# Two layers of a transformer on one core: a new order and new skews for the stages of the token pipeline, and two PSUM banks handed over one by one

## What is computed

```python
h = _layernorm(x, axis=-1) * (1 + ca) + sa
x = x + ga * _L0_attn_ref(h, L0_attn_qkv, L0_attn_wo)            # causal attention, 16 heads
h = _layernorm(x, axis=-1) * (1 + cb) + sb
x = x + gb * _L0_ffn_ref(h, L0_ffn_W_r, ...)                     # r * (relu(k)**2 @ W_v), each token mixed with the one before
...                                                              # the second layer's six vectors
h = _layernorm(x, axis=-1) * (1 + ca) + sa
x = x + ga * _L1_attn_ref(h, L1_attn_Wq, ...)                    # a scan over the tokens, + residual, its own layernorm
h = _layernorm(x, axis=-1) * (1 + cb) + sb
x = x + gb * _L1_ffn_ref(h, L1_ffn_router_w, ...)                # h + shared MLP + the best 2 of 16 experts
```

## Time and profile before

| | before |
|---|---|
| median of 3 runs | 2248.11 us (2240.46 to 2248.99) |
| the profiled execution | 2240.73 us, span 2239.0 us |
| TensorE busy in the span | 1976.6 us (88%) |
| VectorE, ScalarE, GpSimd busy | 1711.7, 1423.5, 927.1 us |
| the token pipeline, first transpose to the first expert's | 1363.68 to 1877.10 us of the span |
| the experts, from there | 361.90 us |

### The profile page before, as it was taken

The page is one execution under the profiler, slowest core; times in us unless marked ns, Lnnn a source line. Parts: engine busy times, 40 slices in busy tenths (PEclk is TensorE's granted clock), DMA queues, the critical chain, the costliest instruction groups (busy, mean ns, idle before and its releaser), DMA issues. The chain is left out here.

```text
span 2239.0 us, 30470 instructions
## 1 busy us (share of the span) xinstructions
PE 1976.6 (88%) x10427; PEld 841.6 (38%) x10427; DVE 1711.7 (76%) x2505; ACT 1423.5 (64%) x1913; POOL 927.1 (41%) x818
## 2 busy tenths in 40 slices
PE   7979999989999999999999995888888766999997
PEld 4442222222222222222222213555555434776775
DVE  6779999999999999999999994567777644333332
ACT  5759999989999889999899992454444211111110
POOL 5853444333334433444333431365554431333423
PEclk9989999999999999999999997999999878999999
DMA  6642311031111221143300001101000022443441
GB/s 206 209 137 43 53 22 32 3 64 22 31 22 31 46 43 31 22 127 117 94 24 13 22 22 44 38 19 48 29 29 28 21 82 75 102 110 97 108 99 24
DMA packets 124926, 133.74 MB, mean 60 GB/s; under 512 B 35289, under 2 KB 119090, under 8 KB 124080
## 3 DMA queue, kind: packets, MB, share of 16 engines
q1 hardware_dynamic: 110192, 117.86, 19.3%
q0 software_dynamic: 14592, 14.08, 3.6%
HBM read 96.85 MB, written 50.63 MB: 66 GB/s over the span
## 5 line engine op out<-in xcount | busy, mean ns | idle before, releaser
L1062 DVE SCALAR_TENSOR_TENSOR arena<-ps_s,arena 128x1024 f32<-128x1024 f32 (+1 forms) x1071 | 1147.1, 1139 | 40.9 <-ACT arena L1028 33.0
L1028 ACT ACTIVATE arena<-ps_s 128x1024 f32<-128x1024 f32 (+1 forms) x1194 | 1041.2, 935 | 115.6 <-PE ps_s L975 103.6
L975 PE MATMUL ps_s<-arena 128*128 128x512 bf16 (+3 forms) x2304 | 607.9, 366 | 87.4 <-DVE arena L1062 69.2
L991 PE MATMUL ps_o<-arena,values 128*32 128x512 f32 (+3 forms) x4608 | 565.7, 568 | 5.2 <-ACT arena L1018 3.9
L1071 POOL TENSOR_SCALAR arena<-arena 128x512 f32<-128x512 f32 x123 | 236.1, 1919 | 514.0 <-ACT arena L1033 513.9
L975 PEld LDWEIGHTS ps_s<-arena 128*128 128x128 bf16 x2304 | 155.1, 97 | 694.0 <-DVE arena L1062 531.3
L1805 ACT ACTIVATE arena<-t_ps_four 128x320 f32<-128x320 f32 (+1 forms) x96 | 42.0, 438 | 322.2 <-PE t_ps_four L1697 322.2
L2130 POOL DMA_INDIRECT out<-values,slot_ids x80 | 123.8, 1547 | 238.2 <-DVE values L2051 209.9
L1697 PE MATMUL t_ps_four<-arena 128*128 128x320 f32 (+1 forms) x768 | 211.0, 434 | 0.6 <-DVE arena L2012 0.6
L991 PEld LDWEIGHTS ps_o<-arena,values 128*32 128x32 f32 x4608 | 94.0, 108 | 233.1 <-issue 185.4
L2024 DVE TENSOR_TENSOR arena<-t_ps_four,arena 128x320 f32<-128x320 f32 (+1 forms) x96 | 47.2, 492 | 168.2 <-ACT arena L1805 168.2
(11 more groups left out here) (203 smaller groups left out, 1762.9 us busy)
## 6 DMA issues: line engine op xcount, KB each, us to landing
arena<-parts_dram SPq DMA_DIRECT2D x320, 64.0 KB, 2.2
parts_dram<-arena SPq DMA_DIRECT2D x32, 384.0 KB, 3.4
arena<-parts_dram SPq DMA_DIRECT2D x24, 512.0 KB, 7.0
slots_in_dram<-in_empty_slots SPq DMA_DIRECT2D x10, 1040.0 KB, 24.8
arena<-slots_in_dram SPq DMA_DIRECT2D x16, 650.0 KB
arena<-in_L_ffn_w_gate SPq DMA_DIRECT2D x16, 352.0 KB, 3.1
arena<-in_L_ffn_w_up SPq DMA_DIRECT2D x16, 352.0 KB, 3.7
arena<-in_L_attn_x SPq DMA_DIRECT2D x8, 512.0 KB, 4.3
```

The lines of the kernel that those rows point to most:

```text
L975: last = pe.matmul(ps_s[:, unit.bank + i, p.at:p.at + p.width], m.k_stack[:, group.g % 2 * HG + p.head, p.kt * P:p.kt * P + P], q_stack[:, ...
L991: last = pe.matmul(ps_o[32 * p.head:32 * p.head + 32, p.w0:p.w0 + p.width], m.values_flat[:, at:at + 32], probs[:, job.at % PROB_BANKS, p. ...
L1028: act.activation(probs[:, unit.slot:unit.slot + n], ps_s[:, unit.bank:unit.bank + n], ACT.Exp, scale=1.0 / DH ** 0.5).then_inc(exped, 1)
L1062: dve.scalar_tensor_tensor(p, ps_s[:, unit.bank:unit.bank + n], 0.0, p, ALU.not_equal, ALU.mult).then_inc(bank, 1)
```

## The change

Three things change in `phase_tokens`. The lists of all four engines have a new order. Some skews are new: `turn_attended` with its modulation and `difference` 1 to 2; `spread` 1, `take_keys` 1 and both scans 3 to 4; `delta_out` 3 to 4; `count`, `choose`, `find_places`, `open_up` 2 and `hide` 2 5 to 6; `rows_final` 4 to 5; `scatter` 5 to 7; `normalise_mixed` 3 to 2. And the two banks of `ps_turn` get a pair of counters each: transposes, `up` products, copies, modulations and the two products of `hide` wait for and hand back one bank at a time. `take_attn` becomes two activations of one bank each, where it was one over both; no other operation is added or removed. New waits keep the single buffer `silu` safe (`open_up` waits for the `hide` before it).

```diff
-    turns = Uses(mixed=3, up0=5, up1=5, attn=0, final=4, up2=5, attended=1)
-    outs = Uses(down=6, attend=1, gate=2, value=2, logits=5, count=5, delta=3)
-    banks = Uses(keys=2, spread0=3, spread1=3)
+    turns = Uses(attended=2, mixed=3, up0=5, up1=5, attn=0, final=4, up2=5)
+    outs = Uses(count=6, delta=4, down=6, attend=1, gate=2, value=2, logits=5)
+    banks = Uses(spread1=4, keys=2, spread0=3)
...
-        turned, turn_taken = sem("turned"), sem("turn_taken")
+        turned = [sem("turned0"), sem("turned1")]
+        turn_taken = [sem("turn_taken0"), sem("turn_taken1")]
...
             def turn(name, b, rows):
-                if turns.before(name, b):
-                    pe.wait_ge(turn_taken, turns.before(name, b))
                 for k in range(KC):
+                    if turns.before(name, b):
+                        pe.wait_ge(turn_taken[k], turns.before(name, b))
                     for t in range(TT):
                         last = pe.transpose(ps_turn[:, k, t * P:t * P + P], rows[:, t, k * P:k * P + P], m.ident[:])
-                last.then_inc(turned, 1)
+                    last.then_inc(turned[k], 1)
...
             def up(b, i):
                 at, width = FM[i]
-                pe.wait_ge(turn_taken, turns.before(f"up{i}", b))
                 for half, w in enumerate((m.s_gate, m.s_up)):
+                    pe.wait_ge(turn_taken[half], turns.before(f"up{i}", b))
                     for k in range(KC):
                         last = pe.matmul(ps_turn[0:width, half], w[:, k, at:at + width], m.h_even[:, k, b * BT:b * BT + BT],
                                          start=k == 0, stop=k == KC - 1)
-                last.then_inc(turned, 1)
+                    last.then_inc(turned[half], 1)
...
             def take_attn(b):
-                act.wait_ge(turned, turns.through("attn", b))
                 if b:
                     act.wait_ge(out_made[1], outs.through("attend", b - 1))
-                act.activation(attnT, ps_turn[:], ACT.Copy).then_inc(turn_taken, 1)
+                for k in range(KC):
+                    act.wait_ge(turned[k], turns.through("attn", b))
+                    act.activation(attnT[:, k], ps_turn[:, k], ACT.Copy).then_inc(turn_taken[k], 1)
 
             def modulate(name, b, out, layer, shift, scale):
-                act.wait_ge(turned, turns.through(name, b))
                 for k in range(KC):
-                    last = act.activation(out[:, k], ps_turn[:, k], ACT.Identity, bias=m.mod_cols[:, layer, shift, k:k + 1],
-                                          scale=m.mod_cols[:, layer, scale, k:k + 1])
-                last.then_inc(turn_taken, 1)
+                    act.wait_ge(turned[k], turns.through(name, b))
+                    act.activation(out[:, k], ps_turn[:, k], ACT.Identity, bias=m.mod_cols[:, layer, shift, k:k + 1],
+                                   scale=m.mod_cols[:, layer, scale, k:k + 1]).then_inc(turn_taken[k], 1)
...
             def open_up(b, i):
                 width = FM[i][1]
-                act.wait_ge(turned, turns.through(f"up{i}", b))
+                if i:
+                    act.wait_ge(turn_taken[1], turns.through(f"up{i - 1}", b))
+                elif b:
+                    act.wait_ge(turn_taken[1], turns.through("up2", b - 1))
+                act.wait_ge(turned[0], turns.through(f"up{i}", b))
                 act.activation(silu[0:width], ps_turn[0:width, 0], ACT.Sigmoid).then_inc(opened, 1)
...
-                then(dve.tensor_tensor(silu[0:width], ps_turn[0:width, 0], silu[0:width], ALU.mult))
+                dve.tensor_tensor(silu[0:width], ps_turn[0:width, 0], silu[0:width], ALU.mult).then_inc(turn_taken[0], 1)
                 if i == 0 and b:
                     dve.wait_ge(out_made[1], outs.through("down", b - 1))
-                dve.tensor_tensor(hidden[0:width, i], ps_turn[0:width, 1], silu[0:width], ALU.mult).then_inc(turn_taken, 1)
+                dve.wait_ge(turn_taken[0], turns.through(f"up{i}", b))
+                dve.wait_ge(turned[1], turns.through(f"up{i}", b))
+                dve.tensor_tensor(hidden[0:width, i], ps_turn[0:width, 1], silu[0:width], ALU.mult).then_inc(turn_taken[1], 1)
...
-            staged([(4, lambda b: ln_1.deviation(pool, b)), (3, rows_mixed), (4, gain), (1, lambda b: ln_c.deviation(pool, b)),
-                    (4, lambda b: ln_e.deviation(pool, b)), (2, lambda b: ln_d.deviation(pool, b)), (4, rows_final), (1, difference),
-                    (5, scatter)])
+            staged([(2, difference), (3, rows_mixed), (4, lambda b: ln_1.deviation(pool, b)), (4, gain), (5, rows_final),
+                    (1, lambda b: ln_c.deviation(pool, b)), (4, lambda b: ln_e.deviation(pool, b)),
+                    (2, lambda b: ln_d.deviation(pool, b)), (7, scatter)])
```

46 lines of the change are left out of this document (25 added, 21 removed).

## The result

The changed kernel takes 2214.27 us (median of 4 runs, 2211.97 to 2216.42), the kernel before beside it 2248.47 (2240.46 to 2248.99): a ratio of 0.9853, 95% interval 0.9832 to 0.9875. That is inside the range of 2166 to 2220, but only in the part of it that was held open for rival 2: the forecast was 2192.0, with 2182 to 2204 as its own range. The profiled execution took 2216.42 us with a span of 2214.7: 24.3 less than before, where 48.7 had been worked out. The medians lie 34.2 apart. The traces show less than that, because the profiled execution of the kernel before is 7.4 us under its median and that of the changed kernel 2.2 over. The pipeline went from 513.4 to 486.0 us (forecast 464.7), the experts from 361.90 to 363.17.

What follows compares the result with a forecast made beforehand. TensorE sets the full ticks' rate (46.83 of 54.18 us busy), latency the first and last stretches. Stretches 46 + 100 + 155.3 + 81.8 + 81.6 = 464.7 against 513.4, 48.7 off 2240.73: 2192.0; range 2166 to 2220, its own 2182 to 2204.

Steps and rivals of the forecast that it cites:

- rival 2: Full ticks: VectorE becomes the bound, paying GpSimd's 11.9 us of long operations; 56 us in five ticks, 2212; chance 0.21.
- Turns and up: Full tick: TensorE's waits between stages sharing banks, and for delta_out and down, fall from 7.35 to 1.3 us; tick 48.1.
- rival 1: Beside find_places: no blocking, small operations slip through, no lost clock; 16 us less, 2176; chance 0.20.
- The stall of delta_out: Ticks 6 to 9: delta_out loses 3.0 us (bounds 0, 6) behind find_places, held up by GpSimd's difference and rows_mixed.
- The 5.7, 10.1 and 5.1 us over the forecast: Forecast stretches: ticks 3 to 5, 100 us; ticks 9 and 10, 81.8; tick 11 to the first expert's rows, 81.6.
- The clock: Ticks with the delta_out stall: it may lower TensorE's clock, 1 us a tick more; bounds 0 and 2.
- The norm chain: Ticks 10 and 11: turn_final waits behind delta_out for a 17.3 us chain, 2.7 and 5.6 us.
- rival 3: Norm chain within one tick decides above 25 us; at 36, ticks 4 to 9 lose 11 each, 2260; chance 0.03.
- tick 10's terms: Tick 10 without mixing: 30.6 us of work, 0.7 of turns and 2.7 of wait, put at 34.5.
- The experts: The 16 experts after the pipeline: untouched by the edit, so their phase stays at 361.9 us.
- The Trainium skill: Cited port rule for VectorE and GpSimd: the loser blocks for the whole instruction; alone it makes the stall 3.0 us or more.

Runs made afterwards that it cites:

- short_after: The changed kernel with GpSimd's six long operations (difference, two of rows_mixed, gain, two of rows_final) cut to 8 or 16 of 256 columns: 2172.97 us, ratio 0.9668.
- short_final: The changed kernel with only GpSimd's gain and the two operations of rows_final cut short: 2197.44 us, ratio 0.9788 to the kernel before.
- short_mixed: The changed kernel with only GpSimd's difference and the two operations of rows_mixed cut short: 2213.20 us, ratio 0.9858 to the kernel before.
- order_only: The kernel before with the new lists, skews and tables, but one pair of counters for both banks: 2254.87 us, ratio 1.0027.

## Why the prediction was right in direction and too large in size

- **Turns and up.** Right. The 7.35 us of waits in a full tick were to become 1.3; without blocking 0.7 is left (47.42 with TensorE busy 46.74). The walk of TensorE's new order held to 4 us in 449 (444.8 measured in short_after), and 2176 for rival 1, no blocking, stood 3 from the 2172.97 of that run. That closeness is in part luck, as the cut also takes GpSimd's own time out of the chains.
- **The stall of delta_out.** Right in place, in cause and in ticks 6 to 9, too large by a third: 2.0 us where 3.0 were worked out. The two products and the scan lost 3.9 us together, not 4.9, since only 0.65 of difference was left when the first of them, the scan at 1572.98, came. The row of L2010 counts six waits, four of them between 1.75 and 2.02; the other two, 0.79 and 1.29 in ticks 10 and 11, were not forecast. The prediction also read the wait before the change from tick 7 alone (0.43) and did not see the 3.50 of ticks 9 and 10.
- **The step that failed: the stall was priced at find_places alone.** The prediction said of it "in the ticks that have both stages (6 to 9); in ticks 3 to 5 there is no count, and in tick 10 and later no difference". But gain and rows_final block mix_again, add_shared and add_delta by the same mechanism, also in ticks that have no find_places: in tick 5 add_delta's two operations took 3.01 and 2.90 us for 1.2 each, in tick 10 add_shared's second took 2.90. Rival 2 had named them; its term never came into the sum. The 5.7, 10.1 and 5.1 us over the forecast go when all the long operations are cut, and then the time falls by 41 us, of which not all is blocking, against the 16 put down for the stall. Up to block 0's count it is mostly gain and rows_final that cost: short_final takes 8.5 us less there than the changed kernel, short_mixed 2.7. For the ticks from 9 on, which half costs how much stays open.
- **The clock.** 1 us a tick was allowed. In ticks 6 to 8 TensorE is busy 143.19 us, and 139.35 in short_after: 1.3 a tick, 2.4 of the 3.8 in tick 7. The size was about right; which stall costs the clock, the traces do not tell.
- **Rival 2** gave 2212, which is nearer to 2214 than the forecast. Its mechanism came in weaker: VectorE did pay for GpSimd, but is busy 45.3 of 53.6 us, and TensorE waits for it at three hand-overs of ps_out; it is not the rate. It had added all 11.9 us of GpSimd; tick 7 shows 7.1 (45.32 against 38.24).
- **The norm chain** (rival 3). turn_final waits for the end of its chain (normalise, L1325) in ticks 10 and 11 alone, 3.22 and 5.85 us, for 2.7 and 5.6 worked out. The mechanism was right, the closeness of the second number partly luck: 17.3 of chain less 10.5 of cover is 6.8, not 5.6. The sums around it do not close either: tick 10's terms give 34.0, not 34.5, and tick 11's 28.7, so its 34.5 holds 5.8 us of low clock that no row prices.
- **The experts** take 1.3 us more and the pipeline starts 1.9 later, neither of them explained; the starts in the traces of the twelve experiments lie between 1363.6 and 1367.3.
- **The Trainium skill** (SBUF — State Buffer, section Terms) lets the loser wait for the whole instruction of the other engine. These traces agree for products of two operands in SBUF, and in both directions: mix_again 4.78 us for 1.48, and gain beside it 2.54 for 2.00. For operations with an operand in PSUM no wait shows (0.68 at 1595.14). Two operands are not the only condition, though: the cast of the earlier trace rows, which also waited, has one.

What stays open: why the halves of the cut give 1 and 17 us and both together 41. In ticks 6 to 8 the halves give 4.1 and 6.0 us and both 14.9; 3.4 of the 4.9 between are in TensorE's busy time, so mainly in the clock. Between block 3's count and block 7's they give 0.2 and 6.0, and both 18.7, and there only 7.8 are found, as the nameless wait. It is open, too, how much of the 41 is GpSimd's own time.

## What to carry to other kernels

When an order is changed, list for every stretch which of VectorE's two-operand SBUF instructions now lie beside long GpSimd instructions, and price all of them, not only those ahead of the wait that you are thinking about. If they can't be moved apart, cut GpSimd's instructions into pieces: moving rows_mixed won nothing here, cutting them in four won 0.8% for 28.5 us more of GpSimd's own time. And measure an order together with the handover that it was made for: this order cost 6 us without it, and the handover was worth some 60 in it once GpSimd's operations were short.

## What the runs showed of the hardware

- Two VectorE products of 64 values a partition (0.23 us each) took 1.85 and 2.04 us, because they had to wait out GpSimd operations of 2.0 us; with those cut into operations of 0.6 us they took 0.47 and 0.56.
- The block is mutual and by whole instructions: GpSimd's gain and rows_final took 2.54, 2.44 and 2.33 us for 2.0 beside mix_again, and two operations of 0.24 and 0.23 took 1.12 and 1.17 beside VectorE's operations of 1.2.
- Giving VectorE 46 us of blocked time back took 41 us off the time in the changed kernel, where no wait of tick 7 but the two behind blocked operations was over 0.32 us, and 49 us took off 17 to 20 in order_only, where TensorE waited for ps_turn as well (VectorE 1748.3 and 1699.2 us busy; 2254.9 to 2234.5, or 1.0027 to 0.9951). Both take GpSimd's own time off too.
- The same two waits of TensorE, about 2.0 and 1.4 us and some 19 us apart, stood in three ticks of the changed kernel; the clock granted was 1.00, 0.97 and 1.00. With one of them left it was 0.97 in three ticks of six, with neither in none of three.
